# Second attention and the ternary feed-forward in one block, one interleaved step per batch

## The reference, cut to what matters

```python
x = x + jnp.tanh(g_xattn[0]) * _L0_xattn_ref(_layernorm(x, axis=-1), ctx_1024, ...)
x = x + jnp.tanh(g_ffn[0]) * _L0_ffn_ref(_layernorm(x, axis=-1), ...)
x = x + jnp.tanh(g_xattn[1]) * _L1_xattn_ref(_layernorm(x, axis=-1), ctx_1024, ctx_1024, ...)
x = x + jnp.tanh(g_ffn[1]) * _L1_ffn_ref(_layernorm(x, axis=-1), ...)

def _L1_xattn_ref(q, k, v, ...):          # 16 heads of 16, 120 keys
    qn = _layernorm(q, qln_g, qln_b)
    scores = jnp.einsum('bqhd,bkhd->bhqk', qh, kh) / np.sqrt(DHEAD)
    attn = jax.nn.softmax(scores, axis=-1)
    y = jnp.einsum('bhqk,bkhd->bqhd', attn, vh).reshape(b, lq, d)
    g = jax.nn.sigmoid(qn @ Wg.T + bg)
    return y * g @ Wo.T

def _L1_ffn_ref(x, w1, conv_w, conv_b, w2):   # hidden 1024
    def act_quant(x):
        scale = 127.0 / jnp.clip(jnp.max(jnp.abs(x), axis=-1, keepdims=True), 1e-05)
        return jnp.clip(jnp.round(x * scale), -128, 127) / scale
    h = bit_linear(x, w1)                 # both operands rounded
    h = depthwise_conv1d(h.transpose(0, 2, 1), conv_w, conv_b)   # three taps along the rows
    h = jax.nn.silu(h.transpose(0, 2, 1))
    return bit_linear(h, w2)
```

## Time and profile before

| | us |
|---|---|
| median of three runs | 1901.86 |
| lowest and highest | 1899.53, 1902.57 |
| the profiled execution, its own time | 1896.22 |
| its span | 1894.4 |
| granted clock, mean | 0.96 |
| PE, DVE, ACT, POOL busy over the span | 87%, 79%, 70%, 54% |

### The profile page before, as it was taken

The page is one execution under the profiler, slowest core; times in us unless marked ns, Lnnn a source line. Parts: engine busy times, 40 slices in busy tenths (PEclk is TensorE's granted clock), DMA queues, the critical chain, the costliest instruction groups (busy, mean ns, idle before and its releaser), DMA issues. The chain is left out here.

```text
span 1894.4 us, 45159 instructions
## 1 busy us (share of the span) xinstructions
PE 1642.1 (87%) x14625; PEld 1340.3 (71%) x14625; DVE 1492.7 (79%) x4215; ACT 1318.3 (70%) x2823; POOL 1017.1 (54%) x1262
## 2 busy tenths in 40 slices
PE   3899999988649999999955999999998587887887
PEld 2677777766448989999953787878886466666666
DVE  5899999999546577655514888888885899999996
ACT  2788888878534444444423777777775699999997
POOL 5468888887734334333337676767650333334331
PEclk9999999999869999999986999999999799999999
DMA  7879989987569787767636676778651121222211
GB/s 231 207 176 209 223 208 215 207 192 199 166 184 228 172 150 181 172 168 172 157 95 103 124 141 134 143 134 143 136 113 48 51 64 55 65 66 66 66 55 46
DMA packets 491989, 268.39 MB, mean 142 GB/s; under 512 B 326143, under 2 KB 481279, under 8 KB 490775
## 3 DMA queue, kind: packets, MB, share of 16 engines
q1 hardware_dynamic: 466135, 230.19, 51.3%
q0 software_dynamic: 24576, 34.62, 9.2%
q10 hardware_dynamic: 1088, 1.11, 0.2%
HBM read 114.20 MB, written 70.11 MB: 97 GB/s over the span
## 5 line engine op out<-in xcount | busy, mean ns | idle before, releaser
L2165 PE MATMUL e_ps_ab<-e_turned,k_w_hi 128*128 128x256 bf16 (+1 forms) x1704 | 285.5, 274 | 25.0 <-DMA e_turned<-e_rows 23.1
L1970 POOL TENSOR_TENSOR e_h_lo<-e_h 128x256 bf16<-128x256 f32 (+1 forms) x213 | 139.5, 659 | 210.7 <-DVE e_h L2071 210.6
L2165 PE MATMUL e_ps_ab<-e_turned,k_w_lo 128*128 128x256 bf16 (+1 forms) x852 | 233.3, 274 | 0.0
L2165 PEld LDWEIGHTS e_ps_ab<-e_turned,k_w_hi 128*128 (+1 forms) x1704 | 177.6, 107 | 40.1 <-issue 25.4
L2002 ACT ACTIVATE e_s<-e_ps_ab 128x256 f32<-128x256 f32 (+1 forms) x213 | 81.1, 382 | 111.1 <-PE e_ps_ab L2165 111.0
L2071 DVE TENSOR_TENSOR e_h<-e_s,e_ps_ab 128x256 f32<-128x256 f32 (+1 forms) x213 | 87.0, 414 | 89.9 <-ACT e_s L2002 87.6
L2546 PE MATMUL f_ps_h<-f_qh,p_arena 128*128 128x256 bf16 x512 | 123.8, 281 | 35.0 <-DVE f_ql L2510 28.4
L2009 ACT ACTIVATE e_yo<-e_ps_y,e_xe 128x256 f32<-128x256 f32 x142 | 59.6, 471 | 116.9 <-PE e_ps_y L2165 114.8
L2546 PE MATMUL f_ps_h<-f_ql,p_arena 128*128 128x256 bf16 x512 | 122.9, 279 | 0.0
L2165 PE MATMUL e_ps_y<-e_w_hi,e_h 128*128 (+1 forms) x426 | 116.4, 273 | 3.7 <-POOL e_h_lo L1970 3.7
L2324 POOL TENSOR_TENSOR f_y<-f_y,f_tmp 128x510 f32<-128x510 f32 x32 | 43.6, 1362 | 136.8 <-DVE f_y L2445 136.8
(11 more groups left out here) (414 smaller groups left out, 6139.5 us busy)
## 6 DMA issues: line engine op xcount, KB each, us to landing
e_xe<-sent_rows SPq DMA_DIRECT2D x71, 272.0 KB, 3.0
back_rows<-e_yo SPq DMA_DIRECT2D x71, 256.0 KB, 2.2
x_rows<-a_x SPq DMA_DIRECT2D x64, 256.0 KB, 3.2
a_xa<-in_x SPq DMA_DIRECT2D x32, 256.0 KB, 3.1
p_arena<-in_xT SPq DMA_DIRECT2D x32, 256.0 KB, 3.5
a_q<-a_mt SPq DMA_DIRECT2D x64, 128.0 KB, 2.5
...
```

The costliest lines, as they stand in the source:

```text
L1970: nc.gpsimd.tensor_tensor(h_lo[0:k, b.par, c, :], h[0:k, b.par, c, :], h_hi[0:k, b.par, c, :], ALU.subtract).then_inc(mg.sem, 1)
L2165: last = nc.tensor.matmul(to, left, right, start=(i == 0), stop=(i == len(terms) - 1))
```

## The change

`attention_second` and `ternary_ffn` become one function `attention_and_ffn` with one step over both. All 43 steps are unrolled.

- The sum of the second attention stays in SBUF (`x1`, four buffers) and is read there by the feed-forward's normalization and by the last addition. The store of `x_rows` and the two loads of it go.
- The rounded hidden rows are no longer turned back by TensorE. The constant is subtracted first, by GpSimd for one half of the rows (`zs0`) and by ScalarE for the other (`zs1`), into bf16 `f_zi`, and one DMA transpose on SP turns both into `f_zq`.
- The feed-forward's PSUM tiles are gone: its pieces share `ps_a` to `ps_e` and `ps_m` with the attention, so waits for the other half's pieces come in. The `1e-5` of the feed-forward's variance is added by VectorE, no more by GpSimd.
- `xa` has five buffers in place of eight.

```diff
-def attention_second(nc, sem, a, pre, src, dst, y_rows, places, halves_c):
+def attention_and_ffn(nc, sem, a, pre, src, dst, y_rows, places, halves_c):
...
-        xa = sb("xa", [P, 8, NT, D], F32)
+        xa = sb("xa", [P, 5, NT, D], F32)
...
-        x1 = sb("x1", [P, 3, NT, D], F32)
+        x1 = sb("x1", [P, 4, NT, D], F32)
...
+        f_zm = sb("f_zm", [P, NT, HID], F32)
+        f_zi = sb("f_zi", [P, J, NT, P], BF16)
+        f_zq = sb("f_zq", [P, J, N], BF16)
...
         def run(step):
-            for n in range(B + 13 - 1):
+            for n in range(B + 12 - 1):
...
-                b = at(8)
-                if b is not None:
-                    dve_out.wait(sp, b, "fin")
-                    nc.sync.dma_start(out_t[b.n], x1[:, b.n % 3, :, :]).then_inc(o_st[b.n % 3], 16)
+                b = at(11)
+                if b is not None:
+                    dve_conv.wait(sp, b, "ffin")
+                    nc.sync.dma_start(out_t[b.n], xo[:, b.par, :, :]).then_inc(o_st[b.n % 3], 16)
+                b = at(9)
+                if b is not None:
+                    act_mlp.wait(sp, b, "zs1")
+                    gp_mlp.wait(sp, b, "zs0")
+                    pe_mlp.wait(sp, at(10), "ym")
+                    nc.sync.dma_start_transpose(f_zq[:, :, :].rearrange("p j (t n) -> p (j t) n", t=NT),
+                                                f_zi[:, :, :, :].rearrange("p j t n -> p (j t n)")).then_inc(z_ld[b.n % 3], 16)
...
+                    act_mlp.wait(gp, b, "qz0")
+                    arrived(gp, z_ld, at(7))
+                    nc.gpsimd.tensor_scalar(f_zi[:, :, 0, :], f_zm[:, 0, :].rearrange("p (j n) -> p j n", j=J), ROUND, None, ALU.subtract).then_inc(gp_mlp.sem, 1)
...
+                    nc.scalar.activation(f_zi[:, :, 1, :], f_zm[:, 1, :].rearrange("p (j n) -> p j n", j=J), ACT.Identity, bias=level[:, 1:2]).then_inc(act_mlp.sem, 1)
+                b = at(6)
+                if b is not None:
+                    gp_mlp.wait(act, b, "right3")
+                    nc.scalar.activation(f_z[:, 4:8, :].rearrange("p j n -> p (j n)"), f_y[:, 4:8, :].rearrange("p j n -> p (j n)"), ACT.Silu).then_inc(act_mlp.sem, 1)
...
+                    dve_conv.wait(dve, b, "iv0")
+                    pe_mlp.wait(dve, b, "ym")
+                    arrived(dve, o_st, at(9))
+                    for t in range(NT):
+                        last = nc.vector.scalar_tensor_tensor(xo[:, b.par, t, :], ps_a[:, t * D:(t + 1) * D], f_inv2[:, b.par, t:t + 1], x1[:, b.n % 4, t, :], ALU.mult, ALU.add)
...
+                    dve_mlp.wait(pe, b, "fql")
+                    dve_out.wait(pe, at(4), "of0")
+                    for j in (4, 5):
+                        last = product(ps_c[:, (j % 2) * N:(j % 2 + 1) * N],
+                                       [(w_q[0][:, c, j * P:(j + 1) * P], x[:, b.par, c, :]) for c in range(KC) for x in (f_qh, f_ql)])
...
+                    dve_out.wait(pe, at(4), "ot")
+                    arrived(pe, c_ld, b)
+                    product(ps_b[0:S, :], halves(chl[:, b.n % 3, 0, :, :], chl[:, b.n % 3, 1, :, :], slice(0, S), wkvh, wkvl, 0, 2 * D)).then_inc(pe_keys.sem, 1)
...
-            attention_second(nc, sem, a, pre, x1, x3, back_rows, places, halves_c)
-            ternary_ffn(nc, sem, a, pre, x3, out)
+            attention_and_ffn(nc, sem, a, pre, x1, out, back_rows, places, halves_c)
```

More of the change, by code:

```diff
@@ new lines, in attention_and_ffn @@
+        dve_mlp = Staged(sem(tag + "dve_mlp"), "fbn:4 fvar:4 fve:4 fxn:4 famax:4 finv:4 fscale:4 fxm:4 fxv:4 fql:4")
+        dve_rows = Staged(sem(tag + "dve_rows"), "bn:1 var:1 ve:1 norm:1")
+        act_probs = Staged(sem(tag + "act_probs"), "ex2:4 raw1:4 raw0:4 ex3:3 ex6:3 ex1:3 ex0:3 ex5:3 ex4:3 ex7:3")
+        act_mlp = Staged(sem(tag + "act_mlp"), "qz1:7 fqh:5 zs1:7 silu1:6 base2:5 silu0:6 tm3:5 base3:5 tm0:5 base0:5 tm1:5 qz0:6 base1:5")
+        act_rows = Staged(sem(tag + "act_rows"), "tanh:3 xt:2 xh:2 q_hi:2 q_hi2:2")
@@ L1373, in step @@
+                if b is not None:
+                    pe_scores.wait(act, b, "sc3")
+                    nc.scalar.activation(probs[0:S, 6:8, :].rearrange("p h n -> p (h n)"), ps_e[0:S, 1, :],
+                                         ACT.Exp, scale=SCALE).then_inc(act_probs.sem, 1)
                     pe_scores.wait(act, b, "sc6")
@@ L1637, in step @@
                     last.then_inc(pe_scores.sem, 1)
-                b = at(9)
+                    act_probs.wait(pe, b, "ex7")
+                    for g in (2, 3):
+                        for j in range(GH):
+                            last = nc.tensor.matmul(ps_e[j * VW:(j + 1) * VW, 1, (g % 2) * N:(g % 2 + 1) * N],
+                                                    v1[0:S, b.par, GH * g + j, :], probs[0:S, GH * g + j, :], start=True, stop=True)
+                    last.then_inc(pe_out.sem, 1)
@@ new lines, in step @@
+                    for g in range(H // GH):
+                        last = nc.tensor.transpose(ps_c[:, g * P:(g + 1) * P], raw[:, b.par, g, 0 * P:1 * P], ident[:, :])
+                    last.then_inc(pe_out.sem, 1)
+                    dve_conv.wait(pe, at(6), "left1")
+                    for g in range(H // GH):
+                        last = nc.tensor.transpose(ps_d[:, g * P:(g + 1) * P], raw[:, b.par, g, 1 * P:2 * P], ident[:, :])
+                    last.then_inc(pe_out.sem, 1)
+                b = at(3)
@@ new lines, in step @@
+                b = at(3)
+                if b is not None:
+                    dve_tops.wait(pe, b, "top5")
+                    for j in range(2):
+                        last = nc.tensor.matmul(ps_m[:, 1, j * 2 * S:(j + 1) * 2 * S], q2[0:96, b.n % 3, 2 + j, 0 * P:1 * P],
+                                                k2[0:96, b.par, 4 + 2 * j:6 + 2 * j, :].rearrange("p j s -> p (j s)"),
+                                                start=True, stop=True)
+                    last.then_inc(pe_tops.sem, 1)
```

1183 lines of the change are left out of this document (493 added, 690 removed).

## The result

The changed kernel takes 1917.76 us (median of 4 runs, 1913.04 to 1918.97), the kernel before in the same comparison 1900.69 (4 runs, 1899.28 to 1902.57): ratio 1.0085, 95% interval 1.0065 to 1.0105. It is slower by 0.9%; I had forecast faster, 1878 us. The profiled execution is the 1918.97, with a span of 1917.2 us.

What follows compares the result with a forecast made beforehand. ACT bounds the joined step: 24.2 us of work plus 1.3 of waits gives T = 25.5; 1157 + 28 T is a 1871 us span, 1873 for the execution, forecast 1878 with 5.6 for the median; 8 in 10: 1842 to 1922.

Steps and rivals of the forecast that it cites:

- the reading of the clock: PE in the second attention, busy 317.85 of 320 us, feed-forward 258.23: granted clock 1.00 in both, so 2.4 GHz kept.
- T: Length of one full step of the joined block, the distance of two `ex2`: forecast 25.5 us, against 25.81 before.
- the table loads: ACT in each joined step: two loads, for the exponentials and `Silu`, 1.31 us each, 2.6 us together.
- The fill: Start of the joined block: steps 4, 5 and 6 lack feed-forward pieces and take 18, 22 and 24 us.
- The drain: End of the joined block: four steps of the last batches at 15, 15, 9 and 15 us, 54 in all.
- ACT's sum: ACT's own work in a joined step, attention, feed-forward and two table loads: 24.2 us, setting the step.
- its wait on `h3`: ACT's `tm3` waits for `h3`, which waits on PE for `top5`: 0.5 us a step.
- the wait for `k_hi`: ACT waits for the keys' product, behind `h2`, `oT` and the gate on PE: 0.3 us a step.
- Rival 3: Each table load on a backlogged ACT costs up to 0.6 us more: T = 26.7, 1912 us; chance 0.05.
- Rival 2: DVE's tail before `fql` stalls beside GpSimd and delays PE: T = 26.2 to 27.9, 1898 to 1946 us; chance 0.18.
- Rival 4: Saved transfers gain nothing; a late SP queue costs `sc3` 0.5 to 1 us a step, T = 26.2, 1898 us; chance 0.09.
- over 270 us beyond the full steps: Sign on the whole block: the forecast is wrong if fill and drain together exceed this, even with T right.

Runs made afterwards that it cites:

- the clock held: Changed kernel plus thirteen idle PE matmuls a step, eight before the first exponential's wait and five before later ones: 1887.51 us, ratio to before 0.9943.
- the one-table kernel: Changed kernel with silu computed through Tanh, so no table loads in the steps, and seven idle products in PE's gaps: 1901.06 us, ratio 1.0024.
- thirteen early products: Changed kernel with thirteen idle PE matmuls early in the step, six before `of0` and seven before `top5`: 1939.62 us, ratio 1.0203.

## Why the prediction was wrong

**The step that failed** is the reading of the clock in the first paragraph, "PE at four fifths of the time kept 2.4 GHz", from which T and the whole block were worked out at full speed. It took an average over 320 us for a guarantee. What the runs show in its place: PE's idle time around the exponentials, with PE at 88% on average, lets the clock fall and makes eleven of 28 steps long; held there, the kernel is 30 us faster and beats the one before. I had priced the table loads on ACT alone, though PE waits for `ex3` behind one of them.

**The fill** was the second failure: 18, 22 and 24 us were guessed from the engines' sums. With the clock held they are 23.3, 23.3 and 25.9. In the first of them ACT waits 4.67 us for the gate's product and 4.55 for q's: a step written in a fixed order keeps its chain of results when the other half's pieces are absent (I read this in the first of the three only). That is 8.5 us, the clock 6.9 more. The drain was 5 us short. Against that the first `ex2` came 6.5 us before the forecast with the clock held, and on time (1042.6) in the changed kernel.

**Steps that held.** T was 25.5 in the forecast and is 25.71 undisturbed; ACT's sum was 24.2 and is 0.956 x 25.71 = 24.6, its wait on `h3` 0.5 and is 0.69, the wait for `k_hi` does not show. Of the 3 us that I took off for three shorter steps, 1.8 came, all in the last (23.96). A table load lasts 1.28 us, backlog or not, and takes 1.40 from start to start, against my 1.31: two of them make up most of the 0.2 us by which T came out longer. Rival 3 had up to 0.6 us more for each, the rows show 0.1, and it falls. The Trainium skill's 2.66 us for a switch ("ScalarE: Activation LUTs", *What ACT_TABLE_LOAD costs*) is contradicted by these rows: behind the load there are 0.01 us, and no 1.38. Rival 2, DVE's tail: its pairs took 0.73 us. PE's weight load did wait 0.7 us a step for `fql`, which I had excluded. Rival 4: the wait of PE for the mask came up twice, 1.6 us in all. `zs0` cost 2.78 us within my bounds of 1 and 3, and was hidden. Turning z by DMA landed after 4.3 to 7.8 us and was hidden.

So the change is worth some 0.5% with the clock held, less than half of the 1.2% forecast, and the clock takes 1.4% back. My range held the time, but by luck: no rival had the clock in it.

**Two slips in the forecast's own figures.** The 5.6 us that I added for the median over the profiled execution did not come: here the median is 1.2 us below the profiled one. And the sign "over 270 us beyond the full steps" could not have warned of anything: from 977 us on, the forecast's own sum has 183 us of fill and drain, and the changed kernel has 204.

**Open.** In the one-table kernel PE waits 1.6 us a step for the small cast and the operation behind it (42 us in 26 waits), elsewhere in the step, and no fall follows. Why a gap there is harmless, these runs do not tell, nor why thirteen early products made 25 long steps out of 11. What lengthens the one-table kernel's drain is open too. Nor do they tell why the block before ends at places 10 us apart from run to run.
